# Sixteen graphs through a GRU graph network on one core: the last rounds of an order written by hand are rewritten, and two final states change the way in which they are turned

## The reference

```python
A = (adj != 0).astype(x.dtype)
h = x
for l in range(5):
    m = h @ weight[l]
    agg = jnp.einsum('bij,bid->bjd', A, m)
    h = gru_cell(agg, h, w_ih, w_hh, b_ih, b_hh)   # r, z, n gates, 128 wide each
x = layernorm(x + h * mask)
for idx, W1, b1, W2, b2 in groups:                 # five lists of nodes below 25
    out = relu(norm_adj @ relu(norm_adj @ x[idx] @ W1 + b1) @ W2 + b2)
    fused[idx] += softmax(fusion_w)[g] * out
x = layernorm(x + fused)
```

## Time and profile before

| | |
|---|---|
| median of 3 runs | 511.0 us (510.79 to 512.11) |
| profiled execution: time | 511.83 us |
| profiled execution: span of the core | 510.0 us |
| PE busy | 492.1 us, 96% of the span |
| DVE busy | 382.4 us, 75% |
| POOL busy | 311.1 us, 61% |
| ACT busy | 300.9 us, 59% |

### The profile page before, as it was taken

One profiled execution on the slowest core, in us unless ns is written; L12 is line 12 of the kernel. 1 busy time (PEld: TensorE's weight loads), 2 busy tenths in 40 slices (PEclk: granted clock), 3 DMA queues, 4 the chain that ended last, 5 costly groups with the idle time before them and its releaser, 6 DMA issues.

```text
span 510.0 us, 7334 instructions
## 1 busy us (share of the span) xinstructions
PE 492.1 (96%) x2393; PEld 240.3 (47%) x2393; DVE 382.4 (75%) x727; ACT 300.9 (59%) x549; POOL 311.1 (61%) x282
## 2 busy tenths in 40 slices
PE   8999999999999999999999999999999999999992
PEld 5344444444444444444555444445544444564462
DVE  3777876687867788997677889876567878556794
ACT  4546655655656566666656665566565556754564
POOL 3654775757775688775777458766444645424564
PEclk9999999999999999999999999999999999999998
DMA  8768253654626446337826466242143251222212
GB/s 266 231 153 174 48 150 60 185 159 105 134 41 166 107 100 166 83 81 148 195 48 145 123 185 168 61 85 41 22 101 62 59 98 41 62 60 62 59 32 83
DMA packets 131610, 55.45 MB, mean 109 GB/s; under 512 B 95140, under 2 KB 123252, under 8 KB 131572
## 3 DMA queue, kind: packets, MB, share of 16 engines
q1 hardware_dynamic: 106336, 31.93, 30.4%
q10 hardware_dynamic: 25236, 23.05, 14.8%
HBM read 27.70 MB, written 4.19 MB: 63 GB/s over the span
## 4 chain that ended last, share of the span: by engine, by line
PE 77%; DVE 14%; ACT 4%; issue 3%; DMA 1%; ACTq 0%; DVEq 0%
PE pA L664 22%; PE pR L671 5%; PE pR L670 5%; PE pR L669 5%; PE pZ L669 5%; PE pZ L671 5%; PE pZ L670 5%; PE pIN L669 3%; PE pIN L671 3%; PE pIN L670 3%; PE pHN L669 3%; PE pHN L671 3%; PE pHN L670 3%; DVE T L1155 2%; DVE T L1159 2%
## 5 line engine op out<-in xcount | busy, mean ns | idle before, releaser
L484 POOL TENSOR_TENSOR HT<-H,HT 128x512 f16<-128x512 f32 x74 | 89.1, 1204 | 109.5 <-ACT HT L959 109.3
L664 PE MATMUL pA<-A,NAT 128*128 128x512 fp8e4 x640 | 151.2, 379 | 0.2 <-DVE A L1144 0.2
L473 POOL TENSOR_TENSOR ZH<-Z,H 128x512 f32<-128x512 f32 x80 | 102.5, 1281 | 38.7 <-ACT Z L972 37.0
L1155 DVE SCALAR_TENSOR_TENSOR T<-pHN,BHN,R 128x512 f32<-128x512 f32 x80 | 59.9, 748 | 74.8 <-ACT R L965 74.4
L976 ACT ACTIVATE pIN<-T,COLS 128x512 f32<-128x512 f32 x80 | 55.4, 692 | 76.5 <-DVE T L1159 76.4
L664 PEld LDWEIGHTS pA<-A,NAT 128*128 128x128 f16 x640 | 62.5, 98 | 72.1 <-DVE A L1144 0.7
L959 ACT ACTIVATE HT<-H 128x512 f16<-128x512 f32 x74 | 46.7, 631 | 64.3 <-DVE H L1168 64.3
L965 ACT ACTIVATE R<-pR,BRZ 128x512 f32<-128x512 f32 x80 | 54.5, 681 | 26.7 <-PE pR L671 26.5
L1164 DVE SCALAR_TENSOR_TENSOR pIN<-Z,pIN 128x512 f32<-128x512 f32 x80 | 55.1, 689 | 18.8 <-ACT pIN L976 18.7
L1150 DVE TENSOR_TENSOR AG<-pA,AG 128x512 f16<-128x512 f32 x80 | 54.7, 684 | 9.0 <-ACT AG L955 8.8
L955 ACT ACTIVATE AG<-pA 128x512 f16<-128x512 f32 x80 | 47.2, 590 | 20.6 <-PE pA L664 17.8
(11 more groups left out here) (217 smaller groups left out, 845.0 us busy)
## 6 DMA issues: line engine op xcount, KB each, us to landing
AS<-in_adj_dram ACTq DMA_DIRECT2D x13, 1024.0 KB, 6.0
XR<-in_x_dram ACTq DMA_DIRECT2D x16, 256.0 KB, 3.0
XS<-in_x_dram ACTq DMA_DIRECT2D x13, 256.0 KB, 3.2
out_dram<-Y SPq DMA_DIRECT2D x16, 192.0 KB, 2.1
AS<-in_adj_dram SPq DMA_DIRECT2D x2, 1024.0 KB, 10.4
AS<-in_adj_dram SPq DMA_DIRECT2D x4, 256.0 KB, 5.4
NAT<-HT SPq DMA_TRANSPOSE x64, 3.1
XS<-in_x_dram SPq DMA_DIRECT2D x3, 256.0 KB, 8.4
```

The costliest lines, as they stand in the source:

```text
L473: g_.tensor_tensor(ZH[:, :], Z[:, :], H[:, b, :], ALU.mult).then_inc(zh_p, 1)
L484: g_.tensor_tensor(HT[:, b, 1, :], H[:, b, :], HT[:, b, 0, :], ALU.subtract).then_inc(h_lo, 1)
L664: last = mm(pA2[:, k % 2, :], NAT[:, k % 2, h, i, :], A8[:, b, i, :], start=(h == 0 and i == 0), stop=(h == 1 and i == NI - 1))
L1155: v.scalar_tensor_tensor(out=T[:, :], in0=pHN[:, :], scalar=BHN[:, 0:1], in1=R[:, :], op0=ALU.add, op1=ALU.mult).then_inc(t_v, 1)
```

## The change

The order of the steps from 55 on is rewritten, so that graphs 9, 10 and 11 have their final steps at 58, 60 and 63 where they had them at 61, 66 and 67. Graphs 13, 14 and 15 start at steps 57, 61 and 62 where they started at 55, 56 and 57. Steps 68 to 79 hold the same graphs and layers as before. `BY_DMA` goes from 10 to 12, so the final states of graphs 10 and 11 are split and turned by DMA. The first stage of the last convolution moves from the middle of step 71 to its start. The steps of casts and loads stay.

```diff
-          (11, 10, 12, 8, 9, 13, 14, 15),
-          (11, 10, 12, 9, 11, 13, 14, 15),
-          (10, 11, 12, 13, 14, 15),
+          (11, 10, 12, 8, 9),
+          (11, 10, 13, 9),
+          (11, 10, 14, 15),
+          (11, 12, 13, 14, 15),
+          (12, 13, 14, 15),
           (12, 13, 14, 15),
           (12, 13, 14, 15)]
-BY_DMA = 10
+BY_DMA = E0 = 12
-           [(71, 1), (72, 0), (72, 1), (73, 0), (73, 1), (74, 0), (75, 1)]]
+           [(71, 0), (72, 0), (72, 1), (73, 0), (73, 1), (74, 0), (75, 1)]]
-E0 = Q * TAIL
+assert E0 == Q * TAIL
```

## The result

The changed kernel takes 513.35 us (median of 9 runs, 512.57 to 515.05) against 511.0 us; the ratio is 1.0039, with a 95% interval of 1.0024 to 1.0055. So it is slower, by some 2 us: inside the range (510.1 to 513.5), 1.2 us above the forecast, and just past the bound of 0.3% that was to separate a change from none. The profiled execution took 512.57 us, the fastest of the nine, for a span of 510.8; before, the profiled one took 511.83 for 510.0. Its first 30 us went 0.7 us faster than in the profile of before, in code that the change doesn't touch, so spans are compared here only by stretches.

The account below looks back on a forecast made before the run. TensorE (PE), busy 96% of the span, was taken as the bound, so only its work and waits count. Terms -0.86 - 1.34 + 3.30 = +1.1 us took 511.0 to 512.1 us; range 510.1 to 513.5.

Parts of the forecast that it names:

- The transposes, -0.86: Two sets of transposes of final states leave PE, 0.43 us each, saving 0.86 us.
- Step 53, -1.34: PE's wait at step 53 goes, as POOL's first_state no longer delays the scales of graph 7; saves 1.34 us.
- margin against natural_lo: Rival at step 53: POOL's natural_lo is ready before the scales, so 1.34 us isn't saved; 513.4 us, chance 0.11.
- Steps 61 to 66, +3.30: Work of graphs 9 to 11 crowds DVE beside the second convolution's additions; PE waits 3.30 us in all.
- What comes at steps 61 to 66: The prediction's section pricing DVE's extra work and lateness in steps 61 to 66, from which PE's waits of 3.30 follow.
- The collision in step 62: POOL's sum of halves of graph 10, right behind its kept share, holds DVE's additions in step 62; 1.1 us added.
- excess: DVE's extra work in a step beyond its plain chain; behind T, 2.86 us forecast for step 62, 1.55 for 63.
- the rival in which the additions win the turn: In step 62 DVE's additions go ahead of POOL's halves; losses 2.20 equal the gains, 511.0 us, chance 0.24.
- The inverse root as a holder: Rival: POOL's inverse root behind the kept share of step 63 also holds DVE, adding 1.1; 513.2 us, chance 0.09.
- What costs nothing, and its cover: Moved first stage, starts at 57, 61, 62 and turn_backs in SP's queue (3.1 us each) were taken as hidden, costing nothing.

Follow-up runs that it names:

- spread: Changed kernel with mask, statistics, variances and scales of graphs 10 and 11 one step later; 514.86 us, ratio 1.0075.
- after_pad: Changed kernel with only 24 already fulfilled waits added ahead in SP's queue; 511.64 us, ratio 1.0002.
- before_s7: Kernel before the change, with the scales of graph 7 at step 54 instead of 53; 514.65 us, ratio 1.0073.
- xr_pad: Changed kernel with the last three residual-row loads at steps 71 to 73 and 24 fulfilled waits ahead in SP's queue; 511.45 us, ratio 1.0004.
- best_pad: Changed kernel: graphs 10 and 11 one step later, residual loads at 71 to 73, convolution's first stage mid-step 71, 24 SP waits; 509.90 us, ratio 0.9971.

## Why the prediction was right, and where it wasn't

The sign was right and the time within the range, but the sum had one term too large and lacked one, and the two made up for each other in part: 1.10 too much against a missing 1.5. That the time lay within the range is in part luck; the bound was 0.15 away, and the same kernel run again took 513.57, outside it. "Slower by over 0.3%" had been given 0.31, less than "within" with 0.60.

- **The transposes, -0.86.** As said: the aggregations of steps 69 and 70 start 5.61 us apart where one set stood before.
- **Step 53, -1.34.** As said, by the mechanism named. The aggregations of steps 53 and 57 start 1.37 us less far apart than before. The margin against natural_lo was 0.38 us: it started at 332.20, and the scales ended at 331.82.
- **Steps 61 to 66, +3.30.** The right place, order and kind of waits; measured 2.20. The aggregations start at 385.29, 391.48, 398.10, 404.06 and 409.93, so the four steps lose 0.58, 1.01, 0.35 and 0.26 us; predicted were 1.19, 1.50, 0.34 and 0.27. Two prices in "What comes at steps 61 to 66" were too high. The collision in step 62 was real but cheaper. From T to L1166 it took 389.37 - 384.91 = 4.46, an excess of 2.22 and not 2.86: the kept share ended earlier after T, so the first addition was held 0.25 less, and the rest of the hold was 0.77 by comparison with spread, not 1.1. And in step 63 the additions weren't held by the kept share, because T itself was late: an excess of 395.97 - 392.66 - 2.24 = 1.07, not 1.55. A late engine arrives after the instruction that would have held it. I had taken holds measured on punctual steps and added them to lateness. (2.20 is also the figure of the rival in which the additions win the turn. That is chance: they were held, as the rows show.)

```profile
387.21 1.45 DVE L1338 SCALAR_TENSOR_TENSOR FU<-S,FU 128x128 f32<-128x128 f32 x2
...
394.04 0.68 DVE L1338 SCALAR_TENSOR_TENSOR FU<-S,FU 128x128 f32<-128x128 f32 x2
...
386.92 1.20 POOL L481 TENSOR_TENSOR YM<-Y 128x512 f32<-128x512 f16 x1
...
393.95 1.18 POOL L501 TENSOR_TENSOR RS<-VE,NHALF 128x5 f32<-128x5 f32 x1
```

- **The inverse root as a holder.** These rows of the timeline after (DVE in steps 62 and 63, POOL beside them) settle that rival: the sum of halves held the two additions, the root, begun 0.09 before two others, did not. The Trainium skill's rule ("SBUF — State Buffer", "Who interferes with whom") agrees with the rows of the sum of halves and not with those of the root.
- **"What costs nothing, and its cover": the step that failed.** It priced the two turn_backs by what they transfer (3.1 us each, beside other work) and by the order of SP's queue, and found both hidden. That was right for them. It didn't price their instructions. With them in the queue, a block of SP's instructions is loaded just as the last transpose is due; the transpose is issued 0.42 late and collides with a load that it used to be ahead of. It cost 1.5 us in the profile, and in the medians 1.9 to 2.3 us (513.57 against 511.64 and 511.25). after_pad shows it: the same kernel, with SP's instructions at another place in their blocks, is level with the kernel before.

Without that term the sum by measured sizes is -0.86 - 1.37 + 2.20 = 0.0, and after_pad's ratio of 1.0002 says the same. So the new order with its DMA turns was a draw, by a stall removed at 53 and another made at 62 to 66, and what made the kernel measurably slower came from SP's added instructions and not from the order of the steps.

What ties the load of instructions to SP's late issue is that the two move together. At the last transpose the gap is 0.42 us in the six profiles that have the load there and under 0.1 in the other eight; and in the three with 24 waits it is 0.41 to 0.43 at an earlier transpose, where the load had gone. What isn't shown is how the one delays the other: the block's packet starts on q14 only at 474.0 us, 0.6 after the issue at 473.39, so its transfer can't have held the issue up. And the loss was never brought about in the kernel before, where six waits missed the place.

## What to carry to other kernels

Where an order is written by hand, a piece of work has a cover on the engine that does it and a deadline at its user; spread and before_s7 each cured a crowded engine and broke a deadline one step further, and only cure and deadline together gave the 0.3%. A step's slack is best written as two bounds, how late each operand may be, before work is put into it. And when a change adds instructions to a queue that is nearly idle, look at what is issued last from that queue onto the critical path, and whether its issue still follows its release.

## What the runs showed of the hardware that wasn't expected

- A load of instructions for the queue that issues DMAs went with a DMA's issue 0.42 us behind its release, where it was 0.07 to 0.09 without. Where padding moved the load 35 us earlier, the issue just before it was late by as much (after_pad, xr_pad, best_pad).
- A DMA transpose whose transfer overlapped a 256 KB load took 4.5 us from issue to landing (4.4 to 4.6 in three profiles); started 0.35 us sooner behind its release, with the same load behind it, 3.1.
- Whether POOL holds DVE depends on the operation and not on its recorded length alone: a sum of halves of 1.20 us did, an inverse root of 1.18 us on 5 elements a row did not.
